# The last batch of an attention loop: values two pairs behind the scores, and its projection split around the last pair

## The chip, the cores and the metric

One core of one Trainium2 chip runs the whole kernel as one program. The metric is device microseconds (us) of one execution. The engines are PE (TensorE matmul; PEld is its weight load), DVE (VectorE), ACT (ScalarE), POOL (GpSimd) and SP (SyncE, which here only issues DMAs). Each works through its own instructions in the order written and waits on semaphores for the others.

## The reference

Two layers over 16 batches of 256 tokens with width 256. The first layer is a conditioned feed-forward block. The second is attention with 16 heads, then a mixture of eight experts. The change is in the attention:

```python
q = _ln(qkv[:, :, 0].transpose(0, 2, 1, 3), qn_g, qn_b)
k = _ln(qkv[:, :, 1].transpose(0, 2, 1, 3), kn_g, kn_b)
v = qkv[:, :, 2].transpose(0, 2, 1, 3)
scores = jnp.einsum('bhnd,bhmd->bhnm', q, k) / jnp.sqrt(jnp.float32(HD))
attn = jax.nn.softmax(scores, axis=-1)
o = jnp.einsum('bhnm,bhmd->bhnd', attn, v)
o = o.transpose(0, 2, 1, 3).reshape(b, n, H * HD)
x = x + o @ Wout.T
tok = x.reshape(-1, d)
gate = jax.nn.softmax(tok @ Wgate.T, axis=-1)
vals, idx = jax.lax.top_k(gate.T, k_cap)
```

The expert choice (`top_k` over all 4096 tokens) needs the gates of every batch, so nothing of the experts can start before the last batch's `x` and its logits are done.

## The kernel before

There are three stages: the first layer (`first_block`), `attention`, and `experts` (which begins with the choice of tokens, called the router here). Each is a block of its own with a barrier between.

`attention` walks over t = -2 to 17. Step t has PAIRS = 8 pair steps s, one for each pair of heads. In pair step s of step t the engines do, for batch t and pair s:

- PE: `scores` (8 matmuls into two score banks, waits for `exped`, the exponentials of the pair before), then `transposes` of the pair before (waits for `shared`), then `values` of that same pair (waits for `pT_act` and `pT_dve`, the two copies of the transposed probabilities).
- DVE: `lowest_of` (the minimum, one per side), `invert` (reciprocal of the sum, one per side), the copy of one transposed bank (`pT_dve`), and `o_l`, the low part of the output.
- ACT: `exps` (four exponentials, each with the read of its accumulator), then the copy of the other transposed bank (`pT_act`), and `o_h`, the high part of the output.
- POOL: `divide` for side 0 and side 1 (`shared`).

Every fp32 product is made of three float32r products of high and low parts (`product`). In earlier steps the holes between these are filled with work of later batches: the products that make q, k and v (`chunk`), and their transposes. For t = 15, the last batch, there is no later batch, so these pair steps hold little else. What one bank `tr` passes through is fixed by a table of slots 0 to 15, two per pair step (`TR_FILLS`, shifted by `TR_LAG`):

```python
TR_FILLS = [("x2", 0, 1), ("gates", 0, 3), ("proj", 0, 4), ("qk", 0, 5), ("qk", 1, 6), ("qk", 2, 7), ("h", 0, 8), ("qk", 3, 9),
            ("proj", 1, 10), ("qk", 4, 11), ("qk", 5, 12), ("qk", 6, 13), ("qk", 7, 14)]
TR_LAG = {"h": 2, "proj": -1, "x2": -2, "gates": -2, "qk": 1}
```

So batch b's output projection (`project`, 24 matmuls for each half n) runs in step b + 1 at s = 2 and s = 5; ACT copies each half to `proj`, POOL adds both halves to the row tile `x2` at s = 6 (`x2_done`), and the transposes of `x2` and the gate products follow in step b + 2. DVE takes the statistics of `x2`, POOL the root, DVE the normalised rows `x2n`, and SP stores them. For batch 15 these are steps 16 and 17, with no scores beside them. Under all of this SP loads 256 KB pieces of expert weights, ACT and DVE split them (`ew_h` at even s, `ew_l` at odd s) and SP stores them again. Batch 15's `x2` tile is first loaded with the rows of the first layer (`x1_again_in`).

Of the kernel before, what the change touches and what calls it, by code (L numbers as in the profile page):

```python
# [23 lines left out]
P = 128  # L24
# [824 lines left out]
def attention(nc, exponent, weights, rows_of, banks, ident, x1_rows, hbias, cols, x2_rows, logit, out, a, halves, sbuf, sems):  # L849
# [4 lines left out]
    with s:  # L854
# [31 lines left out]
        def first(b):  # L886

            return isinstance(b, int) and b == 0

        drained = {"h": out_h, "proj": out_proj, "x2": out_x2, "gates": out_gates, "qk": out_qk}  # L890
# [31 lines left out]
        with nc.Block() as block:  # L922
            @block.sync
            def _(sp):
# [22 lines left out]
                def step(t, odd):  # L947
                    pieces(t, (0,))
                    b = t - 2
                    if live(b):  # L950
                        wait(sp, out_normed, TT, b, TT)
                        sp.dma_start(x2_rows[bass.ds(b * T, T), :].rearrange("(t p) d -> p t d", p=P), x2n[:, :, :]).then_inc(x2n_stored, 16)
                    b = t - 1
                    if live(b):
                        wait(sp, tr_x2, 1, b - 1, 1)
                        wait(sp, x2_stored, 16, b - 1, 16)
                        wait(sp, out_normed, TT, b - 1, TT)
                        sp.dma_start(x2[:, :, :], x1_rows[bass.ds(b * T, T), :].rearrange("(t p) d -> p t d", p=P)).then_inc(x1_again_in, 16)
                    pieces(t, (1,))
                    b = t + 3  # L960
                    if live(b):
                        wait(sp, tr_h, 1, b - 1, 1)
                        sp.dma_start(x1[:, :, :], x1_rows[bass.ds(b * T, T), :].rearrange("(t p) d -> p t d", p=P)).then_inc(x1_in, 16)
                    pieces(t, (2,))
                    b = t - 1
                    if live(b):
                        wait(sp, x2_done, 1, b, 1)
                        sp.dma_start(out[bass.ds(b * T, T), :].rearrange("(t p) d -> p t d", p=P), x2[:, :, :]).then_inc(x2_stored, 16)
                    pieces(t, (3,))
# [6 lines left out]
            def _(pe):  # L976
# [11 lines left out]

                def transposes(b, q):
                    for side in range(2):  # L990
                        wait(pe, shared, H, b, 2 * q + side + 1)
                        for m in range(TT):
                            for n in range(TT):
                                last = nc.tensor.transpose(pT_bank[side][:, m * T + n * P:m * T + (n + 1) * P],  # L994
                                                           prob[q % 2 * 2 + side][:, n, m * P:(m + 1) * P], ident[:, :])
                        last.then_inc(pT_done, 1)

                def values(b, q, its):
                    wait(pe, pT_act, PAIRS, b, q + 1)
                    wait(pe, pT_dve, PAIRS, b, q + 1)  # L1000
                    wait(pe, o_lo, PAIRS, b, q)
                    if q == 0:
                        wait(pe, chunk_out, 12, b, 12)
                    for m in range(TT):
                        for side in range(2):
                            h = 2 * q + side
                            last = nc.tensor.matmul(o_bank[side * HD:(side + 1) * HD, 0:T], v[its][:, m, h * HD:(h + 1) * HD],  # L1007
                                                    pT[q % 2 * 2 + side][:, m, :], start=(m == 0), stop=(m == TT - 1))
# [21 lines left out]
                def fill(t, i):  # L1030
# [7 lines left out]
                    if name == "x2":  # L1038
                        wait(pe, x2_done, 1, b, 1)
                    if name == "gates":  # L1040
# [16 lines left out]
                    if name == "gates":  # L1057
# [4 lines left out]
                        last.then_inc(tr_gates, 1)  # L1062

                def step(t, odd):
                    for s in range(PAIRS):
                        b, q, its = pair_at(t, s, 1, odd)
                        if live(t):
# [8 lines left out]
                        if name == "proj" and live(c):  # L1076
                            project(t, c, n, 1 - odd)
                        if live(b):
                            values(b, q, its)
                        fill(t, 2 * s + 1)  # L1080
# [3 lines left out]
            def _(act):  # L1084
# [10 lines left out]
                def empty(b, name, j, its):  # L1095
# [9 lines left out]
                    if name == "qk":  # L1105
                        wait(act, tr_qk, 8, b, j + 1)
                        if isinstance(b, int) and b == 1:
# [4 lines left out]
                                             bias=cols[:, g + 1:g + 2], scale=cols[:, g:g + 1]).then_inc(out_qk, 1)  # L1112
                    if name == "proj":
                        wait(act, tr_proj, TT, b, j + 1)
# [24 lines left out]
                def step(t, odd):  # L1139
                    for s in range(PAIRS):  # L1140
                        b, q, its = pair_at(t, s, 2, odd)
                        if live(b):
                            wait(act, pv_done, PAIRS, b, q + 1)
                            if q == 0:
                                wait(act, tr_proj, TT, b - 2, TT)
                            nc.scalar.activation(o_h[its][:, q, :], o_bank[:, 0:T], ACT.Copy).then_inc(o_hi, 1)
                        empty(*fill_at(t, 2 * s - 1), 1 - odd)
# [21 lines left out]
            def _(pool):  # L1169
# [18 lines left out]
                def step(t, odd):  # L1188
                    far, new, old = t + 2, t + 1, t - 1
                    for s in range(PAIRS):  # L1190
# [7 lines left out]
                        if live(old) and s == X2_PAIR:  # L1198
                            wait(pool, out_proj, TT, old, TT)
# [14 lines left out]
            def _(dve):  # L1214
# [35 lines left out]
                def out_norm(t, s, part):  # L1250


                    if s == OUT_STATS_PAIR and live(t - 1):
                        if part < TT:
                            wait(dve, x2_done, 1, t - 1, 1)
                            link.note(nc.vector.bn_stats(out_stats[:, part, :], x2[:, part, :]))
# [8 lines left out]
                    if s == OUT_APPLY_PAIR and live(t - 2) and part < TT:  # L1265
                        wait(dve, out_root, 1, t - 2, 1)
# [20 lines left out]
                def step(t, odd):  # L1287
                    far = t + 2
                    for s in range(PAIRS):
                        i = 2 * s  # L1290
                        before = chunks_at(t, s - 1)
                        if live(t):
                            lowest_of(t, s, 0)
                            lowest_of(t, s, 1)
                        b, q, its = pair_at(t, s, 2, odd)
                        if live(b):
                            wait(dve, o_hi, PAIRS, b, q + 1)
                            nc.vector.tensor_tensor(o_l[its][:, q, :], o_bank[:, 0:T], o_h[its][:, q, :].bitcast(F32), ALU.subtract).then_inc(o_lo, 1)
                        if live(t):
# [516 lines left out]
```

## Time and profile before

| | us |
|---|---|
| median of 3 runs | 1573.68 (1571.06 to 1573.81) |
| the profiled execution's own time | 1573.23 |
| span of its trace | 1571.3 |
| scores of batch 15, pair 1, begin | 1217.82 |
| `x2` of batch 15 complete (DVE's statistics begin) | 1279.44 |
| first router instruction on DVE | 1284.89 |

The span is what the trace covers. The execution's own time is 1.93 us longer. Times of an instruction are from the span's start. The page gives the granted TensorE clock as a share of full speed: 1.00 is 2.4 GHz, 0.50 is 1.2 GHz.

### The profile page before, as it was taken

The page shows a single profiled execution, that of the slowest core. Times are in us where ns is not written, and L with a number is a line of the kernel's source. Part 1 is how long each engine was busy: PE and PEld are TensorE (multiplying, and loading weights), DVE is VectorE, ACT ScalarE, POOL GpSimd, SP SyncE. Part 2 cuts the span into 40 slices and gives each one's busy share as a digit, 9 for nine tenths or more (in the row PEclk, how much of TensorE's full clock was granted, in tenths as well). Part 3 has the DMA queues.
Part 4 walks back from the last instruction along what each step waited for, and adds up shares of the span by engine and source line. Part 5 has one row for each costly group of instructions (what it writes and reads, how often), then busy time and mean ns, then how long its engine had stood idle before and what let it go on. Part 6 is the DMA issues. An engine that isn't in the chain of part 4 may idle for free. (4 is left out here: it accounts for less than half of the span.)

```text
span 1571.3 us, 31208 instructions
## 1 busy us (share of the span) xinstructions
PE 1390.1 (88%) x9672; PEld 1138.5 (72%) x9672; DVE 1019.1 (65%) x2493; ACT 960.7 (61%) x2537; POOL 783.9 (50%) x737
## 2 busy tenths in 40 slices
PE   1599999997899999999999999999998752599996
PEld 1589999995567777777777777777776542498996
DVE  2686667644677776777777677767766446565642
ACT  2266655564777777777877877787776510335452
POOL 1376666653345545654564565556545310255633
PEclk9799999998999999999999999999999875699999
DMA  7122222210122222222221222222222234067652
GB/s 233 41 65 67 63 71 61 54 42 27 41 67 80 83 63 76 87 81 75 80 82 60 74 87 81 81 74 88 75 68 81 81 126 165 27 201 226 207 170 27
DMA packets 92408, 138.90 MB, mean 88 GB/s; under 512 B 8656, under 2 KB 61824, under 8 KB 92160
## 3 DMA queue, kind: packets, MB, share of 16 engines
q1 hardware_dynamic: 83600, 126.02, 24.2%
q0 software_dynamic: 6144, 8.39, 2.9%
q10 hardware_dynamic: 2544, 3.16, 0.6%
q8 instruction: 42, 0.69, 0.2%
q14 instruction: 78, 0.64, 0.1%
HBM read 87.20 MB, written 50.35 MB: 88 GB/s over the span
## 5 line engine op out<-in xcount | busy, mean ns | idle before, releaser
L1182 POOL TENSOR_TENSOR prob<-prob,share_p 128x512 f32<-128x512 f32 x256 | 268.0, 1053 | 342.0 <-DVE share_p L1285 342.0
L1091 ACT ACTIVATE prob<-bank,shift 128x256 f32<-128x256 f32 x512 | 236.0, 474 | 115.4 <-DVE shift L1279 115.2
L1279 DVE TENSOR_REDUCE shift<-bank 128x2 f32<-128x512 f32 x256 | 164.7, 685 | 207.4 <-PE bank L984 202.2
L1177 POOL TENSOR_TENSOR raw_qk<-raw_qk,rq 128x512 f32<-128x512 f32 x128 | 145.5, 1149 | 65.3 <-DVE rq L100 65.3
L1007 PE MATMUL bank<-pT,v 128*64 128x256 f32 x1024 | 141.1, 397 | 36.0 <-ACT pT L1154 35.1
L147 PE MATMUL bank<-wqkv_h,rowsT_h 128*128 128x512 f32 x384 | 161.1, 420 | 4.3 <-PEq L392 3.5
L147 PE MATMUL bank<-wqkv_h,rowsT_l 128*128 128x512 f32 x384 | 152.2, 396 | 0.0
L147 PE MATMUL bank<-wqkv_l,rowsT_h 128*128 128x512 f32 x384 | 151.9, 396 | 0.0
L984 PE MATMUL bank<-landing 64*128 64x256 f32 x1024 | 149.2, 411 | 0.4 <-ACT prob L1091 0.4
L994 PEld LDWEIGHTS bank<-ident,prob 128*128 128x128 f32 x1024 | 111.1, 142 | 44.5 <-issue 42.8
L994 PE MATMUL bank<-ident,prob 128*128 128x128 f32 x1024 | 142.2, 282 | 0.4 <-POOL prob L1182 0.4
L1007 PEld LDWEIGHTS bank<-pT,v 128*64 128x64 f32 x1024 | 62.8, 137 | 93.5 <-ACT pT L1154 42.1
L984 PEld LDWEIGHTS bank<-landing 64*128 64x128 f32 x1024 | 90.4, 191 | 32.5 <-issue 24.6
L1110 ACT ACTIVATE landing<-bank,cols 128x512 f32<-128x512 f32 x128 | 102.3, 799 | 11.0 <-PE bank L1050 11.0
L1091 ACT ACTIVATION_READ_ACCUMULATOR prob<-bank,shift 128x1 f32 x512 | 104.2, 204 | 0.0
L630 POOL TENSOR_TENSOR hid_l<-hid,hid_h 128x512 fp32r<-128x512 f32 x64 | 86.0, 1353 | 32.4 <-ACT hid_h L547 31.7
L1132 ACT ACTIVATE raw_sq<-bank 128x512 f32<-128x512 f32 x128 | 79.4, 620 | 30.0 <-DVE ssq L1275 30.0
L543 ACT ACTIVATE hid<-bank,cols 128x256 f32<-128x256 f32 x128 | 53.4, 471 | 68.9 <-PE bank L147 68.9
L1275 DVE TENSOR_REDUCE ssq<-raw_sq 128x8 f32<-128x512 f32 x128 | 86.1, 675 | 6.2 <-ACT raw_sq L1132 4.6
L1305 DVE COPY pT<-bank 128x512 f32<-128x512 f32 x128 | 88.0, 688 | 0.4 <-issue 0.3
L1050 PE MATMUL bank<-ident,raw_qk 128*128 128x128 f32 x512 | 81.8, 283 | 5.8 <-ACT landing L1110 4.4
L147 PEld LDWEIGHTS bank<-wqkv_h,rowsT_h 128*128 128x128 f32 x384 | 73.4, 191 | 18.1 <-issue 4.0
(279 smaller groups left out, 4052.7 us busy)
## 6 DMA issues: line engine op xcount, KB each, us to landing
ew_raw<-in_fc1s SPq DMA_DIRECT2D x32, 256.0 KB, 3.3
split_w1h<-ew_h SPq DMA_DIRECT2D x32, 256.0 KB, 2.0
split_w1l<-ew_l SPq DMA_DIRECT2D x32, 256.0 KB, 2.5
ew_raw<-in_fc2s SPq DMA_DIRECT2D x32, 256.0 KB, 2.9
split_w2h<-ew_h SPq DMA_DIRECT2D x32, 256.0 KB, 2.1
split_w2l<-ew_l SPq DMA_DIRECT2D x32, 256.0 KB, 2.6
ew_h<-split_w1h SPq DMA_DIRECT2D x8, 1024.0 KB
ew_l<-split_w1l SPq DMA_DIRECT2D x8, 1024.0 KB
```

Source lines behind the costliest of these rows:

```text
L147: last = nc.tensor.matmul(out, a, b, start=(n == 0), stop=(n == 3 * len(ks) - 1))
L630: nc.gpsimd.tensor_tensor(hid_l[:, 2 * g:2 * g + 2, :], hid[:, 2 * g:2 * g + 2, :], hid_h[:, 2 * g:2 * g + 2, :].bitcast(F32), ALU.subtrac ...
L984: mm = nc.tensor.matmul(score_bank[side][:, n * T:(n + 1) * T], qT[odd][r, s, n * P:(n + 1) * P], kT[odd][r, s, :], start=True, stop=True)
L994: last = nc.tensor.transpose(pT_bank[side][:, m * T + n * P:m * T + (n + 1) * P], prob[q % 2 * 2 + side][:, n, m * P:(m + 1) * P], ident[: ...
L1007: last = nc.tensor.matmul(o_bank[side * HD:(side + 1) * HD, 0:T], v[its][:, m, h * HD:(h + 1) * HD], pT[q % 2 * 2 + side][:, m, :], start= ...
L1091: last = nc.scalar.activation(prob[at][:, n, :], score_bank[side][:, n * T:(n + 1) * T], ACT.Exp, bias=shift[:, at, n:n + 1], scale=-1.0, ...
L1110: nc.scalar.activation(dst[its][:, j % 2 * 4:j % 2 * 4 + 4, j // 4 * P:(j // 4 + 1) * P], tr[:, :].rearrange("p (m n) -> p m n", m=4), ACT ...
L1177: nc.gpsimd.tensor_tensor(part, part, rq[:, n, c * 8:(c + 1) * 8].unsqueeze(2).to_broadcast([P, 8, HD]), ALU.mult).then_inc(normed, 1)
L1182: nc.gpsimd.tensor_tensor(prob[at][:, :, :], prob[at][:, :, :], share[:, at, :].unsqueeze(2).to_broadcast([P, TT, T]), ALU.mult).then_inc( ...
L1275: nc.vector.tensor_reduce(ssq[:, n, c * 8:(c + 1) * 8], raw_sq[c % 2][:, :].rearrange("p (h d) -> p h d", h=8), AX, ALU.add).then_inc(summ ...
L1279: nc.vector.tensor_reduce(shift[:, s % 2 * 2 + side, :], score_bank[side][:, :].rearrange("p (n m) -> p n m", n=TT), AX, ALU.min).then_inc ...
L1305: nc.vector.tensor_copy(pT[q % 2 * 2 + 1][:, :, :].rearrange("p m n -> p (m n)"), pT_bank[1][:, :]).then_inc(pT_dve, 1)
```

## The change

Only batch 15 (`closing`) and the steps 16 and 17 behind it change.

1. `values` of batch 15 run two pair steps behind the scores, not one. Odd pairs write to `chunk_bank[1]`, even ones to `o_bank`; a bank's next write waits for `o_l` of two pairs before. `transposes` gets an explicit wait for both copies of the pair before, which `values` used to imply. `o_h` and `o_l` follow one pair step later (`taken_at`).
2. Step 16 on PE is written out (`finish`). The projection of batch 15 goes to two banks of its own (`last_proj`), both halves n, for pairs 0 to 5 before the values of pair 7, then pair 6, then pair 7.
3. DVE adds each half straight from PSUM to `x2`; the two copies on ACT and the add on POOL are gone for batch 15. The normalised rows of batch 14 move ahead from s = 2 to s = 1 of step 16.

```diff
+def values_at(t, s, odd):
+    if isinstance(t, int) and t == NB - 1:
+        return [(t - 1, PAIRS - 1, 1 - odd)] if s == 0 else [(t, s - 2, odd)] if s > 1 else []
+    return [pair_at(t, s, 1, odd)]
+
+def taken_at(t, s, odd):
+    if isinstance(t, int) and t == NB - 1:
+        return [pair_at(t, s, 2, odd)] if s < 2 else [(t, s - 3, odd)] if s > 2 else []
+    if isinstance(t, int) and t == NB:
+        return [(t - 1, q, 1 - odd) for q in {0: (PAIRS - 3, PAIRS - 2), 2: (PAIRS - 1,)}.get(s, ())]
+    return [pair_at(t, s, 2, odd)]
...
+        last_proj = chunk_bank[0], score_bank[0]
+        def values_bank(b, q):
+            return chunk_bank[1] if closing(b) and q % 2 else o_bank
...
                 def transposes(b, q):
+                    if isinstance(b, int) and b == NB - 1:
+                        wait(pe, pT_act, PAIRS, b, q)
+                        wait(pe, pT_dve, PAIRS, b, q)
...
                 def values(b, q, its):
-                    wait(pe, o_lo, PAIRS, b, q)
+                    wait(pe, o_lo, PAIRS, b, max(q - 1, 0) if closing(b) else q)
...
+                def project_last(ks, its):
+                    for n in range(TT):
+                        for k in ks:
+                            if n == 0:
+                                wait(pe, o_lo, PAIRS, NB - 1, k + 1)
+                            oh, ol = (o[its][:, k, n * P:(n + 1) * P] for o in (o_h, o_l))
+                            for i, (l, r) in enumerate(((oh, wo_h), (oh, wo_l), (ol, wo_h))):
+                                last = nc.tensor.matmul(last_proj[n][:, 0:D], l, r[:, k, :], start=(k == 0 and i == 0),
+                                                        stop=(k == PAIRS - 1 and i == 2))
+                        if k == PAIRS - 1:
+                            last.then_inc(tr_proj, 1)
...
+                def finish(t, its):
+                    fill(t, 1)
+                    values(t - 1, PAIRS - 2, its)
+                    transposes(t - 1, PAIRS - 1)
+                    wait(pe, exped, H, t - 1, H)
+                    project_last(range(PAIRS - 2), its)
+                    fill(t, 3)
+                    values(t - 1, PAIRS - 1, its)
+                    project_last((PAIRS - 2,), its)
+                    project_last((PAIRS - 1,), its)
...
+                        if closing(t - 1) and s == 3:
+                            wait(dve, x1_again_in, 16, t - 1, 16)
+                            for n in range(TT):
+                                wait(dve, tr_proj, TT, t - 1, n + 1)
+                                nc.vector.tensor_tensor(x2[:, n, :], last_proj[n][:, 0:D], x2[:, n, :], ALU.add).then_inc(out_proj, 1)
```

**PE, pair step s = 1 of step 15.** The transposes of pair 0 (`bank<-ident,prob`), then before the change its values (`bank<-pT,v`), the gate products of batch 13 and the scores of pair 2:

```order
L994 MATMUL bank<-ident,prob 128x128 [waits shared]
L994 MATMUL bank<-ident,prob 128x128 x3
L994 MATMUL bank<-ident,prob 128x128 [waits shared]
L994 MATMUL bank<-ident,prob 128x128 x3
L1007 MATMUL bank<-pT,v 64x256 [waits o_lo,chunk_out,pT_dve,pT_act]
L1007 MATMUL bank<-pT,v 64x256 x3
L1060 MATMUL bank<-wgate,proj 128x8 [waits out_x2]
L1060 MATMUL bank<-wgate,proj 128x8 x3
L984 MATMUL bank<-landing 128x256 [waits exped]
L984 MATMUL bank<-landing 128x256 x3
```

The same place after the change:

```order
L1032 MATMUL bank<-ident,prob 128x128 [waits shared,pT_dve,pT_act]
L1032 MATMUL bank<-ident,prob 128x128 x3
L1032 MATMUL bank<-ident,prob 128x128 [waits shared]
L1032 MATMUL bank<-ident,prob 128x128 x3
L1112 MATMUL bank<-wgate,proj 128x8 [waits out_x2]
L1112 MATMUL bank<-wgate,proj 128x8 x3
L1019 MATMUL bank<-landing 128x256 [waits exped]
L1019 MATMUL bank<-landing 128x256 x3
```

The values are gone from between the transposes and the next scores. They stand one pair step later, behind the next transposes, and the transposes name two more semaphores.

**PE, the end of step 15 and the start of step 16.** Before, the values of pair 6, the transposes and values of pair 7, then the transposes of batch 14's `x2` and its gates:

```order
L1007 MATMUL bank<-pT,v 64x256 [waits o_lo,pT_dve,pT_act]
L1007 MATMUL bank<-pT,v 64x256 x3
L994 MATMUL bank<-ident,prob 128x128 [waits shared]
L994 MATMUL bank<-ident,prob 128x128 x3
L994 MATMUL bank<-ident,prob 128x128 [waits shared]
L994 MATMUL bank<-ident,prob 128x128 x3
L1007 MATMUL bank<-pT,v 64x256 [waits o_lo,pT_dve,pT_act]
L1007 MATMUL bank<-pT,v 64x256 x3
L1055 MATMUL bank<-ident,x 128x128 [waits out_proj,x2_done]
L1055 MATMUL bank<-ident,x 128x128 x3
L1060 MATMUL bank<-wgate,proj 128x8 [waits out_x2]
L1060 MATMUL bank<-wgate,proj 128x8 x3
```

After, the values of pair 5, the transposes of `x2`, the values of pair 6 and the transposes of pair 7, up to the first projection matmuls of batch 15 (`bank<-wout_h,o_h`):

```order
L1045 MATMUL bank<-pT,v 64x256 [waits o_lo,pT_dve,pT_act]
L1045 MATMUL bank<-pT,v 64x256 x3
L1107 MATMUL bank<-ident,x 128x128 [waits out_proj,x2_done]
L1107 MATMUL bank<-ident,x 128x128 x3
L1045 MATMUL bank<-pT,v 64x256 [waits o_lo,pT_dve,pT_act]
L1045 MATMUL bank<-pT,v 64x256 x3
L1032 MATMUL bank<-ident,prob 128x128 [waits shared,pT_dve,pT_act]
L1032 MATMUL bank<-ident,prob 128x128 x3
L1032 MATMUL bank<-ident,prob 128x128 [waits shared]
L1032 MATMUL bank<-ident,prob 128x128 x3
L1064 MATMUL bank<-wout_h,o_h 128x256 [waits o_lo,exped]
L1064 MATMUL bank<-wout_l,o_h 128x256
```

Values come a pair later: those of pair 6 stand behind batch 14's `x2` transposes. 36 projection matmuls follow the transposes of pair 7 instead of its values.

**DVE, step 16.** Before, up to the statistics of batch 15's rows, which wait for POOL's add (`x2_done`):

```order
L1298 TENSOR_TENSOR o_l<-bank,o_h 128x256 [waits o_hi]
L1305 COPY pT<-bank 128x512 [waits pv_done,pT_done]
L1298 TENSOR_TENSOR o_l<-bank,o_h 128x256 [waits o_hi]
L1268 TENSOR_SCALAR x2n<-x,out_moment,out_rstd 128x256 [waits x2n_stored,out_root] x2
L1256 BN_STATS out_stats<-x 128x6 [waits x2_done] x2
L1261 BN_AGGR out_moment<-out_stats 128x2 [waits att_links]
L1261 BN_AGGR out_moment<-out_stats 128x2
```

After, with the two adds from PSUM (`x<-bank,x`) on DVE itself:

```order
L1365 TENSOR_TENSOR o_l<-bank,o_h 128x256 [waits o_hi] x2
L1377 COPY pT<-bank 128x512 [waits pv_done,pT_done]
L1335 TENSOR_SCALAR x2n<-x,out_moment,out_rstd 128x256 [waits x2n_stored,out_root] x2
L1365 TENSOR_TENSOR o_l<-bank,o_h 128x256 [waits o_hi]
L1370 TENSOR_TENSOR x<-bank,x 128x256 [waits tr_proj,x1_again_in]
L1370 TENSOR_TENSOR x<-bank,x 128x256 [waits tr_proj]
L1323 BN_STATS out_stats<-x 128x6 [waits out_proj] x2
L1328 BN_AGGR out_moment<-out_stats 128x2 [waits att_links]
L1328 BN_AGGR out_moment<-out_stats 128x2
```

The statistics now wait for DVE's own adds (`out_proj`), each of which waits for its half of the projection (`tr_proj`).

## Rows read from the trace of the kernel before

**Rows 1.** Page: span and PE; chain that ended last, first piece (start us, us).

```profile
span 1571.3 us, 31208 instructions
PE 1390.1 (88%) x9672; PEld 1138.5 (72%) x9672; DVE 1019.1 (65%) x2493; ACT 960.7 (61%) x2537; POOL 783.9 (50%) x737
...
1349.22 0.30 issue
```

**Rows 2.** Windows of PE, one pair step each: length, busy, clock, DMA share, GB/s.

```profile
1217.82:1225.57 7.75, 5.54 (x33) 0.80 0.28 88
1225.57:1233.32 7.75, 7.75 (x49) 0.75 0.18 56
1233.32:1238.70 5.38, 3.17 (x27) 1.00 0.12 42
...
1257.27:1279.44 22.17, 15.97 (x102) 0.86 0.14 48
sum 61.62, PE 46.59; mean PE 6.66
```

**Rows 3.** Timeline of PE, pair steps 1 and 3: start us, us, instruction, [idle before].

```profile
1217.82 1.14 PE L984 MATMUL bank<-landing 64*128 64x256 f32 x8
...
1233.32 1.13 PE L984 MATMUL bank<-landing 64*128 64x256 f32 x8
1234.38 1.09 PE L994 MATMUL bank<-ident,prob 128*128 128x128 f32 x8
1237.68 1.08 PE L1007 MATMUL bank<-pT,v 128*64 128x256 f32 x8 [2.21 <-ACT pT L1154]
```

**Rows 4.** Timelines of DVE, ACT and POOL, pair steps 3, 4 and 7.

```profile
1234.48 1.29 DVE L1279 TENSOR_REDUCE shift<-bank 128x2 f32<-128x512 f32 x2 [3.19 <-PE bank L984]
...
1261.84 0.74 DVE L1256 BATCH_NORM_STATS2 out_stats<-x 128x6 f32<-128x256 f32 x2
...
1235.21 0.47 ACT L1091 ACTIVATE prob<-bank,shift 128x256 f32<-128x256 f32 x1 [1.39 <-DVE shift L1279]
...
1236.93 0.21 ACT L1091 ACTIVATION_READ_ACCUMULATOR prob<-bank,shift 128x1 f32 x1
1237.02 0.61 ACT L1154 ACTIVATE pT<-bank 128x512 f32<-128x512 f32 x1
...
1236.51 2.49 POOL L1182 TENSOR_TENSOR prob<-prob,share_p 128x512 f32<-128x512 f32 x2 [4.09 <-DVE share_p L1285]
1241.89 2.04 POOL L1182 TENSOR_TENSOR prob<-prob,share_p 128x512 f32<-128x512 f32 x2 [2.89 <-DVE share_p L1285]
```

**Rows 5.** Timeline of PE, pair steps 4 and 5, at half clock.

```profile
1243.06 1.98 PE L1007 MATMUL bank<-pT,v 128*64 128x256 f32 x8 [2.21 <-ACT pT L1154]
1244.97 1.84 PE L984 MATMUL bank<-landing 64*128 64x256 f32 x8
```

**Rows 6.** Timeline of PE, pair step 5: first of 24 projection matmuls, then the values.

```profile
1247.59 0.37 PE L147 MATMUL bank<-wout_h,o_h 128*128 128x256 f32 x1
...
1250.61 1.08 PE L1007 MATMUL bank<-pT,v 128*64 128x256 f32 x8
```

**Rows 7.** Timelines of PE, DVE and POOL behind pair 7's scores.

```profile
1265.56 1.08 PE L1007 MATMUL bank<-pT,v 128*64 128x256 f32 x8 [0.88 <-DVE pT L1305]
...
1268.01 1.03 PE L1060 MATMUL bank<-wgate,proj 128*128 128x8 f32 x8 [0.78 <-ACT proj L1119]
...
1267.09 0.42 DVE L1298 TENSOR_TENSOR o_l<-bank,o_h 128x256 fp32r<-128x256 f32 x1 [1.64 <-ACT o_h L1146]
...
1279.44 0.75 DVE L1256 BATCH_NORM_STATS2 out_stats<-x 128x6 f32<-128x256 f32 x2 [11.28 <-POOL x L1201]
...
1278.15 1.26 POOL L1201 TENSOR_TENSOR x<-proj,x 128x512 f32<-128x512 f32 x1 [13.06 <-ACT proj L1116]
```

**Rows 8.** Timelines of SP and DVE: rows loaded for batch 15, the router's start.

```profile
1268.68 0.41 SPq L958 DMA_DIRECT2D x<-x_rows  x1
...
1284.89 0.42 DVE L1445 TENSOR_REDUCE peak<-logit 128x32 f32<-128x256 f32 x1 [2.65 <-PEq L922]
```

More of the change, by code:

```diff
@@ L888, in first, with closing, wait_x2 @@
             return isinstance(b, int) and b == 0
+        last_proj = chunk_bank[0], score_bank[0]
+        def closing(b):
+            return isinstance(b, int) and b == NB - 1
+        def values_bank(b, q):
+            return chunk_bank[1] if closing(b) and q % 2 else o_bank
+        def wait_x2(eng, b):
+            if closing(b):
+                wait(eng, out_proj, TT, b, TT)
+            else:
+                wait(eng, x2_done, 1, b, 1)
         drained = {"h": out_h, "proj": out_proj, "x2": out_x2, "gates": out_gates, "qk": out_qk}
@@ L1006, in values @@
                             h = 2 * q + side
-                            last = nc.tensor.matmul(o_bank[side * HD:(side + 1) * HD, 0:T], v[its][:, m, h * HD:(h + 1) * HD],
+                            last = nc.tensor.matmul(values_bank(b, q)[side * HD:(side + 1) * HD, 0:T], v[its][:, m, h * HD:(h + 1) * HD],
                                                     pT[q % 2 * 2 + side][:, m, :], start=(m == 0), stop=(m == TT - 1))
@@ L1038, in fill @@
                     if name == "x2":
-                        wait(pe, x2_done, 1, b, 1)
+                        wait_x2(pe, b)
+                        if closing(b):
+                            wait(pe, out_gates, 1, b - 1, 1)
                     if name == "gates":
@@ L1062, in fill @@
                         last.then_inc(tr_gates, 1)
+                def finish(t, its):
[8 more added lines that the diff above has]
+                    project_last((PAIRS - 1,), its)
                 def step(t, odd):
+                    if isinstance(t, int) and t == NB:
+                        finish(t, 1 - odd)
+                        return
                     for s in range(PAIRS):
-                        b, q, its = pair_at(t, s, 1, odd)
+                        b, q, _ = pair_at(t, s, 1, odd)
                         if live(t):
@@ L1077, in step @@
                             project(t, c, n, 1 - odd)
-                        if live(b):
-                            values(b, q, its)
+                        for b, q, its in values_at(t, s, odd):
+                            if live(b):
+                                values(b, q, its)
                         fill(t, 2 * s + 1)
@@ L1112, in empty @@
                                              bias=cols[:, g + 1:g + 2], scale=cols[:, g:g + 1]).then_inc(out_qk, 1)
-                    if name == "proj":
+                    if name == "proj" and not closing(b):
                         wait(act, tr_proj, TT, b, j + 1)
@@ L1140, in step @@
                     for s in range(PAIRS):
[L1141 to L1146, printed above, removed]
+                        for b, q, its in taken_at(t, s, odd):
+                            if live(b):
+                                wait(act, pv_done, PAIRS, b, q + 1)
+                                if q == 0:
+                                    wait(act, tr_proj, TT, b - 2, TT)
+                                nc.scalar.activation(o_h[its][:, q, :], values_bank(b, q)[:, 0:T], ACT.Copy).then_inc(o_hi, 1)
                         empty(*fill_at(t, 2 * s - 1), 1 - odd)
@@ L1197, in step @@
                             nc.gpsimd.tensor_tensor(rstd[:, :], var_eps[:, :], exponent[:, :].to_broadcast([P, TT]), ALU.pow).then_inc(spread_out, 1)
-                        if live(old) and s == X2_PAIR:
+                        if live(old) and not closing(old) and s == X2_PAIR:
                             wait(pool, out_proj, TT, old, TT)
@@ L1254, in out_norm @@
                         if part < TT:
[L1255 removed]
+                            wait_x2(dve, t - 1)
                             link.note(nc.vector.bn_stats(out_stats[:, part, :], x2[:, part, :]))
@@ L1264, in out_norm @@
                             nc.vector.tensor_scalar(out_var[:, :], out_moment[:, :, 1], LN_EPS, None, ALU.add).then_inc(out_spread, 1)
-                    if s == OUT_APPLY_PAIR and live(t - 2) and part < TT:
+                    if s == (1 if closing(t - 1) else OUT_APPLY_PAIR) and live(t - 2) and part < TT:
                         wait(dve, out_root, 1, t - 2, 1)
@@ L1294, in step @@
                             lowest_of(t, s, 1)
[L1295 to L1298, printed above, removed]
+                        for b, q, its in taken_at(t, s, odd):
+                            if live(b):
+                                wait(dve, o_hi, PAIRS, b, q + 1)
+                                nc.vector.tensor_tensor(o_l[its][:, q, :], values_bank(b, q)[:, 0:T], o_h[its][:, q, :].bitcast(F32), ALU.subtract).then_inc(o_lo, 1)
+                        if closing(t - 1) and s == 3:
[3 more added lines that the diff above has]
+                                nc.vector.tensor_tensor(x2[:, n, :], last_proj[n][:, 0:D], x2[:, n, :], ALU.add).then_inc(out_proj, 1)
                         if live(t):
```

2 lines of the change are left out of this document (1 added, 1 removed).

## The prediction

> **What bounds the kernel now.** The page comes first: PE is busy 88% of 1571.3 us, more than any other engine, but the chain that ended last reaches back only to 1349.22 [rows 1]. It says nothing of the attention, so the stretch that is changed has to be read by itself. The front gives the fixed points. From the router's first DVE instruction at 1284.89 [rows 8] to the end of the span are 286.41 us that the change leaves alone. The router needs the last logits and the last stored rows, so whatever batch 15 gains in front of it moves the end by as much.
>
> The windows of PE give batch 15. From the scores of pair 1 at 1217.82 to the complete `x2` at 1279.44 are 61.62 us, in which PE is busy 46.59 [rows 2]. The reader is to see three things. Pair step 3, which holds nothing extra and runs at full clock, takes 5.38 us with PE busy for 3.17. The steps with gates or a projection take 7.75. The tail from pair 7's scores on takes 22.17.
>
> Why 5.38? The timelines of one pair step show it. Scores start at 1233.32 [rows 3], the minimum at 1234.48, the exponentials at 1235.21, and the last accumulator read ends at 1236.93 + 0.21 = 1237.14, which is 3.82 after the scores began. Only then does ACT copy the transposed bank, ending at 1237.02 + 0.61 = 1237.63 [rows 4], and 0.05 later the values start, after PE waited 2.21 [rows 3]. The next scores stand behind the values in PE's order. So the loop is scores, minimum, exponentials, copy, values. PE isn't short of time. Its order makes the scores wait for a copy that they don't need.
>
> **The change part by part.** I follow PE in absolute time S, the start of each pair's scores, first at full clock.
>
> *Ordinary pair steps.* With the values of the pair before last, whose copies are long done, the next scores wait only for the exponentials: 3.82 + 0.05 (the semaphore's delay seen above) = 3.87 in place of 5.38. PE must fit into it. Scores take 1.06 (1233.32 to 1234.38 [rows 3]). In the new order pair 4's scores would have begun at 1237.14 + 0.05 = 1237.19. Side 1 of pair 3's transposes needs the second divide, which ends at 1236.51 + 2.49 = 1239.00 [rows 4], 1.81 later. Half the transposes is 0.55, and values are 1.02 (5.38 less 4.36, the values' start). That is 1.81 + 0.55 + 1.02 = 3.38, so 0.49 is spare. Where no weight split runs beside POOL, two divides take 2.04 and more is spare. The added wait for copies costs nothing: they end 0.49 after the exponentials, while scores take 1.06. Queued behind that wait are the values, which have the same slack. The gates of step 1 (1.03 [rows 7]) fill a hole that was a wait.
>
> *Steps with half of batch 14's projection.* Here PE's own work is longer than the loop. 24 matmuls take 1250.61 - 1247.59 = 3.02 [rows 6]. Pair step 2: 1.81 + 0.55 + 3.02 + 1.02 = 6.40. Pair step 5 has the shorter divides before it. They end at 1241.89 + 2.04 = 1243.93 [rows 4], 1.41 after their exponentials (1238.70 + 3.82 = 1242.52), so side 1 goes right behind side 0: 1.06 + 1.09 + 3.02 + 1.02 = 6.19.
>
> *Sum to pair 7.* From S1 = 1217.82: +3.87 (S2), +6.40 (S3), +3.87, +3.87 (S5), +6.19 (S6), +3.87 gives S7 = 1245.89.
>
> *The tail.* Values of pair 6 start at S7 + 4.36, when their copies are done. They take 1.02 and transposes of pair 7 1.09, which makes 6.47. The two statistics of batch 14 (0.74) delay pair 7's second divide to about S7 + 5.97 (1243.93 - 1238.70 = 5.23, and 0.74 [rows 4]), when side 0 of the transposes is just done: nothing. Then 36 matmuls at 3.02/24 = 4.53, at S7 + 11.00. Gates of batch 14: 1.03. Values of pair 7, then `o_h` on ACT and `o_l` on DVE: 1265.56 to 1267.51, 1.95 [rows 7], with pair 6's six matmuls hidden under the two. With 0.05 for the semaphore, S7 + 14.03. Pair 7's six matmuls: 0.13 apart and 0.28 for the last give 0.91. Each add on DVE from PSUM is new; the nearest row is `o_l`, of the same shape and also from PSUM, 0.42. The first hides under the second half's matmuls. So `x2` is complete at S7 + 14.03 + 0.91 + 0.05 + 0.42 + 0.05 = S7 + 15.46 = 1261.35. The old hand-over, a copy on ACT and POOL's 1.26 [rows 7], is gone. Bounds of an add: it can't be below nothing, nor above POOL's 1.26 for both halves, so -0.4 to +0.8.
>
> *Moved work.* The normalised rows of batch 14 go ahead on DVE, and behind them SP loads batch 15's rows (issued at 1268.68 before [rows 8]). In the new order DVE reaches them behind pair 7's copy, about S7 + 8, and the load is issued 0.5 later. The adds want it near S7 + 14, so nothing; if this cover were gone, each microsecond late would cost one. The pieces of expert weights keep their places in the pair steps. ACT's `ew_h` may wait for its piece in the shorter steps. Behind it stand only `o_h` and the next exponentials, which have over 1 us, and the steps concerned (5 and 7) are bound by PE or by the tail. I take nothing, bound 1. Instructions on PE are the same in number.
>
> *Clock.* 1279.44 - 1261.35 = 18.09 at full clock. Before, the granted clock was 0.75 to 0.86 of full in the windows with gates or the tail and 1.00 in pair step 3 [rows 2], so some falls to 1.2 GHz lie in the old 61.62. At half clock, after a wait of 2.21, values took 1.98 and scores 1.84 where they take 1.08 and 1.13 at full [rows 5, 3]: one such fall costs 1.66. The new order has no such waits inside the pair steps, but it has the gates in steps 1 and 2, the small waits of the tail, and the projection in step 2 right behind. I take one fall left on PE's chain: 18.09 - 1.66 = 16.4. Bounds: none, and three (5.0).
>
> The Trainium skill, page "TensorE: Matmul & The Clock Gate", section on HAM oscillation, says that idle gaps between bursts throttle the clock, and that closing them keeps it full. By that rule alone no fall would be left and the sum would be 18.1; this is a rival below. The trace agrees that falls follow waits, but also shows 0.75 in the window in which PE is never idle [rows 2], so the row leaves one.
>
> The skill's page "SBUF — State Buffer", section "SBUF: two separate sides", says a DVE instruction with two SBUF inputs and a GpSimd one exclude each other for the whole instruction. By that the split on DVE could hold a divide back by more than the 0.45 in the rows (2.49 against 2.04), and PE's 0.49 spare could run out. The sum goes by the row.
>
> **Sum.** 1573.23 (the profile's own time, 0.03% below the median of 1573.68) less 16.4 gives 1556.8.
>
> **The rivals.**
>
> - *As worked out*, one or two falls of the clock: 1555 to 1559. Chance 0.50.
> - *Clock full throughout*: 1573.23 - 18.1 = 1555.1, or a little less where the tail's last gates gain too. For it: the waits of 2.21 are gone. Against it: pair step 2. Chance 0.20.
> - *Clock falls three times*: 1573.23 - 18.1 + 5.0 = 1560.1. For it: gates leave PE at half clock in the old steps 1 and 2. Chance 0.13.
> - *The pair step doesn't shorten* since another wait takes the place of the copy: the second divide, or ACT behind a late weight piece. Then four steps stay 1.51 longer each, and the gain is 18.1 - 1.7 - 6.0 = 10.4: 1562.8. Against it: 0.49 and more are spare. Chance 0.10.
> - *It doesn't do what it says*, no change: something else than `x2` holds the router back, such as the stores of expert weights. Against it: DVE's statistics waited 11.28 for `x2` [rows 7] with DVE and ACT nearly idle. Chance 0.04.
> - *Slower*: PE stays at 1.2 GHz from pair 1 to `x2`. Then PE's own work counts. Rows 5 against rows 3 give 1.84/1.13 and 1.98/1.08, about 1.75 times as long. Six steps of 3.17 become 33.3, the two halves of the projection 10.6, and the tail 15.46 + 0.75 x 10.6 (what of it is PE's) = 23.4: 67.3 for 61.62, so 1578.9. Half clock costs about 0.5 us for each microsecond of it on PE's chain, so it decides from some 36 of the 43.5 new ones. Against it: PE ran at full clock through pair step 3, with a wait in it. Chance 0.03.
>
> **How the numbers follow.** Predicted is the likeliest, 1556.8. The first three hold 0.83 between 1554 and 1561; with the bounds on the adds, on `ew_h` and on unseen semaphore delays the range is 1554.0 to 1561.5. About 0.2%, 3 us, is what a measurement of this kernel tells from no change. Faster by more: all but the last two cases, 0.93; within: 0.04; slower: 0.03.
>
> **What would show it.** In the trace after: scores of pairs 3 and 4 3.9 apart, with no PE wait for the ACT copy in between; scores of pair 3 about 6.4 behind those of pair 2; pair 7's scores near 1246 to 1248; 36 projection matmuls in one run at 0.13 each; DVE's adds near 0.42; statistics of batch 15 near 1261 to 1263; the router's start 5.45 behind them as now. The prediction is wrong if PE waits for the second divide, if the granted clock stays at 0.5 for long, if the adds wait for the load of rows, or if router and experts take other than 286.4.

## The result

| | us |
|---|---|
| before, median of 4 runs | 1572.37 (1570.52 to 1573.81) |
| after, median of 4 runs | 1554.24 (1553.39 to 1556.56) |
| ratio after / before | 0.9875 (95% interval 0.9852 to 0.9898) |
| span of the profiled execution, before / after | 1571.3 / 1551.9 |

The change made the kernel faster by 18 us, clearly more than a measurement can miss. The ratio is not the quotient of the two medians, which is 0.9885 and lies inside the interval. The forecast was 1556.8, in a range from 1554.0 to 1561.5. The median lies 0.2 us above the range's lower bound; 0.9875 of the 1572.37 would be 1552.7, below it. So the direction and the wait that was named hold, and the gain was forecast too small: 16.4 us, where the two profiled executions differ by 1573.23 - 1554.05 = 19.2.

The page of the changed kernel answers to [rows 1]:

```profile
span 1551.9 us, 31212 instructions
PE 1380.8 (89%) x9672; PEld 1132.0 (73%) x9672; DVE 1019.5 (66%) x2495; ACT 959.8 (62%) x2535; POOL 783.3 (50%) x736
```

The windows of PE, one for each pair step, then the tail, the end of the stage, and router with experts, answer to [rows 2]. Columns: from:to, length, busy, granted clock, DMA share, GB/s:

```profile
1217.17:1221.05 3.88, 2.95 (x26) 1.00 0.00 0
1221.05:1227.34 6.29, 6.16 (x48) 1.00 0.48 161
1227.34:1231.22 3.88, 3.17 (x26) 1.00 0.25 83
1231.22:1235.10 3.88, 3.39 (x25) 1.00 0.51 173
1235.10:1241.08 5.98, 5.98 (x49) 1.00 0.11 42
1241.08:1244.95 3.87, 3.17 (x26) 1.00 0.75 236
1244.95:1259.97 15.02, 13.82 (x108) 1.00 0.20 71
1259.97:1265.41 5.44, 1.72 (x12) 0.71 0.27 96
1265.41:1551.90 286.49, 217.03 (x1528) 0.85 0.49 152
```

From pair 1's scores to the statistics of batch 15 (called the stretch from here on) are 1259.97 - 1217.17 = 42.80 us, where they were 61.62: 18.82 less. The pair step that took 5.38 takes 3.88. The rest of the 19.4 between the two spans is 0.65 in front of the stretch (1217.82 to 1217.17). What lies behind it is as long as before, 5.44 + 286.49 against 5.45 + 286.41. And the clock reads 1.00 in all seven windows of the stretch in this trace.

PE's timeline of one pair step shows what bounds it now:

```profile
1231.22 1.13 PE L1019 MATMUL bank<-landing 64*128 64x256 f32 x8 [0.71 <-ACT prob L1158]
1232.29 1.45 PE L1032 MATMUL bank<-ident,prob 128*128 128x128 f32 x8
1233.66 1.08 PE L1045 MATMUL bank<-pT,v 128*64 128x256 f32 x8
1235.10 1.13 PE L1019 MATMUL bank<-landing 64*128 64x256 f32 x8 [0.35 <-ACT prob L1158]
```

The wait of 2.21 for ACT's copy [rows 3] is gone. What is left is a wait for the exponentials (`prob`) in front of the scores, 0.35 to 0.93, four times in the stretch. The transposes at 1232.29 take 1.45 for 1.09: their second side waits inside the group for POOL's second divide, which ends at 1233.02, and the later wait is shorter by as much (0.35 for 0.71). PE's spare time beside a weight split is this 0.35, where the prediction had 0.49.

The tail, on PE and DVE, answers to [rows 7]:

```profile
1249.32 1.08 PE L1045 MATMUL bank<-pT,v 128*64 128x256 f32 x8 [0.61 <-ACT pT L1221]
1250.33 1.09 PE L1032 MATMUL bank<-ident,prob 128*128 128x128 f32 x8
1251.18 0.37 PE L1064 MATMUL bank<-wout_h,o_h 128*128 128x256 f32 x1
...
1255.54 0.95 PE L1112 MATMUL bank<-wgate,proj 128*128 128x8 f32 x8
1256.42 1.08 PE L1045 MATMUL bank<-pT,v 128*64 128x256 f32 x8
...
1258.45 0.39 PE L1064 MATMUL bank<-wout_h,o_h 128*128 128x256 f32 x1
...
1257.97 0.42 DVE L1365 TENSOR_TENSOR o_l<-bank,o_h 128x256 fp32r<-128x256 f32 x1 [4.79 <-ACT o_h L1213]
1259.18 0.76 DVE L1370 TENSOR_TENSOR x<-bank,x 128x256 f32<-128x256 f32 x2 [0.78 <-PE bank L1064]
1259.97 0.75 DVE L1323 BATCH_NORM_STATS2 out_stats<-x 128x6 f32<-128x256 f32 x2
```

The 36 projection matmuls run from 1251.18 to 1255.54 without a hole. Pair 7's six begin at 1258.45, as soon as DVE's low part is there. Two adds from PSUM take 0.76, the first beside the second half's matmuls.

### The profile page after: what moved, and what is told of

Read it like the earlier page. It is cut to its first block and busy times, and to the rows that moved or that the text cites. A ratio compares the mean times of both kernels' runs of the same rounds, so it can differ in the third digit from the quotient of the medians.

```text
span 1551.9 us, 31212 instructions
## 1 busy us (share of the span) xinstructions
PE 1380.8 (89%) x9672; PEld 1132.0 (73%) x9672; DVE 1019.5 (66%) x2495; ACT 959.8 (62%) x2535; POOL 783.3 (50%) x736
```

## The experiments

The first theory was that two things had been mixed in one number: PE's order (the copy in front of the scores), and a clock that falls because of the waits this order makes. The rival was that falls (of the granted clock from 1.00 to 0.50) come by chance whatever the order, and that the full clock after the change was luck. A second rival was that the split projection, not the lag of the values, gave most of the gain. All stretches below are from one profiled execution of each kernel; times are medians, ratios are against runs of the kernel before on the same chip. The experiments ran on two chips (`proj_warm` and `both` on the second), beside 11, 10 and 9 runs of before with medians of 1573.59, 1575.85 and 1574.61.

| kernel | pair 1 to 7 | tail | stretch | median us | ratio (95%) |
|---|---|---|---|---|---|
| before | 39.45 | 22.17 | 61.62 | 1572.37 | |
| after | 27.78 | 15.02 | 42.80 | 1554.24 | 0.9875 (0.9852 to 0.9898) |
| after_again | 27.75 | 15.01 | 42.76 | 1554.07 | 0.9873 (0.9836 to 0.9909) |
| lag_only | 28.68 | 20.38 | 49.06 | 1559.39 | 0.9909 (0.9890 to 0.9928) |
| proj_only | 43.21 | 18.04 | 61.25 | 1565.58 | 0.9964 (0.9943 to 0.9986) |
| before_warm | 34.38 | 19.71 | 54.09 | 1566.93 | 0.9948 (0.9926 to 0.9970) |
| proj_warm | 34.46 | 15.46 | 49.92 | 1561.66 | 0.9920 (0.9890 to 0.9949) |
| copy_add | 27.74 | 16.25 | 43.99 | 1555.09 | 0.9881 (0.9861 to 0.9900) |
| one_bank | 27.95 | 19.04 | 46.99 | 1557.44 | 0.9891 (0.9855 to 0.9926) |
| split_scores | 26.64 | 15.14 | 41.78 | 1553.63 | 0.9866 (0.9839 to 0.9893) |
| early_proj | 28.82 | 13.73 | 42.55 | 1554.08 | 0.9868 (0.9840 to 0.9896) |
| both | 27.76 | 13.88 | 41.64 | 1554.95 | 0.9874 (0.9849 to 0.9899) |

**Each part alone.** `lag_only` keeps the first edit and takes back the split and the adds:

```diff
-                    wait(pe, exped, H, t - 1, H)
-                    project_last(range(PAIRS - 2), its)
                     fill(t, 3)
                     values(t - 1, PAIRS - 1, its)
-                    project_last((PAIRS - 2,), its)
-                    project_last((PAIRS - 1,), its)
+                    project(t, t - 1, 0, its)
+                    project(t, t - 1, 1, its)
...
```

> Only the values two pairs behind the scores, with the two banks in turn. The projection of batch 15 stays whole behind pair 7's values, copied by ACT and added by POOL. If PE's order made the scores wait for the copy, pair steps 3 and 4 are 3.88 us as after the change, pair 1's scores to pair 7's scores take 27.8 (39.45 before), and the stretch from pair 1's scores to the statistics of batch 15 takes about 46 (61.62 before, 42.80 after), so about 1557 us. If most of the gain came from the projection's split instead, pair steps stay near 5.4 and the stretch is near 56.

The time is 14.2 us below the 1573.59 of before beside it. The pair steps behind the first are those of after. The stretch, expected at about 46, is 3 us longer: the clock was down twice, at pair 1's scores (window 1217.92 to 1222.70, clock 0.81, 4.78 us for 3.88) and in the tail with the projection (0.92), and the gates waited 0.83 for ACT.

`proj_only` keeps the split and the adds, and puts the values back to one pair behind:

```diff
 def values_at(t, s, odd):
     if isinstance(t, int) and t == NB - 1:
-        return [(t - 1, PAIRS - 1, 1 - odd)] if s == 0 else [(t, s - 2, odd)] if s > 1 else []
+        pass
     return [pair_at(t, s, 1, odd)]
...
```

`taken_at` goes back as well, and all values write to `o_bank` again.

> Only the projection of batch 15 in two banks with six parts ahead of the last values, and the adds on DVE; values stay one pair behind. Pair steps stay 5.38 or more; behind pair 7's scores the tail is near 15.8 us in place of 22.2, the stretch about 55, and the time about 1566 us. If the split's six parts only move work that was not on the path, the tail stays above 20.

The median is as expected. The stretch was not: 61.25 for 55. The profiled execution was the second longest of its seven (1573.44, where they range from 1564.32 to 1574.25), and its windows say why. First two pair steps:

```profile
1217.82:1226.62 8.80, 6.59 (x33) 0.69 0.26 80
1226.62:1235.51 8.89, 8.89 (x50) 0.64 0.23 69
```

The order in these pair steps is that of before, where they took 7.75 each, yet they are 1.1 us longer, and the clock is 0.11 lower. This is the first row that shows the clock as a thing that varies from run to run while the waits are there. The tail is 4.1 shorter than before, 18.04 for the expected 15.8, at a clock of 0.83.

**The clock by itself.** `before_warm` is the kernel before with work for PE in its waits, and nothing else. In an ordinary pair step 0.77 of the 2.21 is left idle (5.37 long, 4.60 busy):

```diff
                 def values(b, q, its):
+                    if isinstance(b, int) and b == NB - 1 and q not in (1, 4):
+                        if q == 0:
+                            wait(pe, chunk_out, 12, b, 12)
+                        for i in range(12 if q < PAIRS - 1 else 4):
+                            nc.tensor.matmul(chunk_bank[1][:, 0:D], wo_h[:, i % 8, 0:P], wo_h[:, i % 8, :], start=True, stop=True)
```

> The kernel before, with 12 extra matmuls (256 columns, into a bank nobody reads) on PE in each wait for the copy in batch 15, four in the last, none where a projection stands there. They fit into the wait of 2.21 us (12 x 0.13 = 1.5), so the order of the work is that of before and only PE's idleness is gone. If the falls of the clock came from those waits, the granted clock stays near 1.00, ordinary pair steps are all 5.4, and the stretch is 55 to 57 us for 61.62: 5 to 6 us faster. If the falls have nothing to do with the waits, the stretch stays 60 to 63 and the time is that of before.

64 matmuls were added and the kernel became faster by 0.5%; the stretch gained 7.5 us where 5 to 6 were expected. Its windows:

```profile
1219.04:1225.40 6.36, 5.59 (x45) 1.00 0.12 44
1225.40:1231.35 5.95, 5.95 (x49) 1.00 0.35 105
1231.35:1236.73 5.38, 4.60 (x39) 1.00 0.28 79
1236.73:1242.10 5.37, 4.60 (x38) 1.00 0.44 146
1242.10:1248.05 5.95, 5.95 (x50) 1.00 0.06 22
1248.05:1253.42 5.37, 4.60 (x38) 1.00 0.56 174
1253.42:1273.13 19.71, 15.04 (x118) 1.00 0.16 54
```

Pair steps are 5.37 and 5.38, the length of the old order, all at full clock. So the order costs 5.38, and the falls had cost 61.62 - 54.09 = 7.5 us of the old stretch in the traced execution. From pair 2's scores to pair 7's scores the rival of chance falls is out: all eight traces of the new order read 1.00 there.

Chance is left at pair 1's scores, which still have the wait of 2.21 in pair step 0 in front of them. Five of the eight traces of the new order read 1.00 in that window, two met half clock (0.81 in `lag_only`, 0.79 in `early_proj`) and one in part (`both`, 0.96). Up to that window `early_proj` has the same order on PE as after, and this is its row:

```profile
1216.89:1221.71 4.82, 3.90 (x25) 0.79 0.00 0
```

So the same wait was followed by a fall in one execution and by none in another, and such a fall cost 0.9 us (4.82 and 4.78 for 3.88).

`proj_warm` adds the same matmuls to `proj_only` (to pairs 0, 2, 3, 5 and 6):

```diff
...
+                    if isinstance(b, int) and b == NB - 1 and q not in (1, 4, PAIRS - 1):
...
+                        for i in range(12):
...
```

> The split projection and DVE's adds alone, values one pair behind, with 12 extra matmuls in each wait for the copy where no projection stands. If proj_only lost its gain only to falls of the clock, all windows up to pair 7's scores read 1.00, those pair steps together take 34.4 us as in before_warm (43.2 in proj_only's trace), the tail is 15 to 16, and the stretch about 50: 4 us less than before_warm's 54.1, at about 1563. If splitting itself makes pair steps longer, they stay above 36 with a full clock.

As expected: 34.46 and 15.46 at clock 1.00. Now the 18.82 us can be laid out in a row, each term the difference of two traces. The falls cost 7.5 (before to `before_warm`), the split with the adds gives 54.09 - 49.92 = 4.2, and the values' lag gives 49.92 - 42.80 = 7.1.

**The adds.** `copy_add` is the changed kernel with ACT's copies and POOL's add:

```diff
-                    if name == "proj" and not closing(b):
+                    if name == "proj":
...
-                        nc.scalar.activation(proj[:, j, :], tr[:, 0:D], ACT.Copy).then_inc(out_proj, 1)
+                        nc.scalar.activation(proj[:, j, :], (last_proj[j] if closing(b) else tr)[:, 0:D], ACT.Copy).then_inc(out_proj, 1)
...
```

> The changed kernel, but with the halves of batch 15's projection copied by ACT and added by POOL as before. By the rows the hand-over then takes 0.05 + 0.39 + 0.1 + 1.26 + 0.03 = 1.8 us for 0.55: the stretch is 1.3 us longer than after, 44.1, all behind the last projection matmul. If POOL's add was hidden, nothing changes.

The stretch is 1.19 longer than after, for 1.3 expected. POOL and DVE at its end:

```profile
1261.23 1.26 POOL L1265 TENSOR_TENSOR x<-proj,x 128x512 f32<-128x512 f32 x1 [8.09 <-ACT proj L1180]
...
1262.52 0.75 DVE L1320 BATCH_NORM_STATS2 out_stats<-x 128x6 f32<-128x256 f32 x2 [2.81 <-POOL x L1265]
```

So 1.2 of the 4.2 are the adds, and 3.0 is left for the six parts ahead. The medians (1555.09 and 1554.24) can't tell this 1.2 from nothing.

**The second bank.** `one_bank` lets every pair's values use `o_bank`:

```diff
-            return chunk_bank[1] if closing(b) and q % 2 else o_bank
+            return o_bank
...
-                    wait(pe, o_lo, PAIRS, b, max(q - 1, 0) if closing(b) else q)
+                    wait(pe, o_lo, PAIRS, b, q)
```

> The changed kernel with one bank for the values of batch 15: each waits for the low part of the pair before. DVE has that part about 2.9 us behind the scores' start in the trace of after (1.29 for the minimum and 0.42 for the low part behind 1.16), values start about 2.2 to 2.4 behind it, so they wait some 0.5 us, ending near 3.9, just what the pair step has. I expect pair steps 3.9 to 4.0 in place of 3.88, steps with a projection unchanged, and the stretch 0 to 0.5 us longer. If the second bank matters, pair steps go to 4.3 or more and the time by 2 us.

Right for the pair steps, wrong for the stretch, which is 4.2 us longer for 0 to 0.5 expected. In the pair steps the values wait 0.78 for DVE's low part, which moves the next scores by only 0.06. But the values of pair 6 wait 2.18:

```profile
1230.98 1.08 PE L1045 MATMUL bank<-pT,v 128*64 128x256 f32 x8 [0.78 <-DVE o_l L1365]
...
1252.62 0.70 PE L1045 MATMUL bank<-pT,v 128*64 128x256 f32 x2 [2.18 <-DVE o_l L1365]
...
1250.58 0.96 DVE L1331 TENSOR_SCALAR out_var<-out_moment 128x2 f32<-128x2 f32 x1
1251.46 0.68 DVE L1406 TENSOR_TENSOR ew_l<-ew_raw,ew_h 128x512 fp32r<-128x512 f32 x1
1252.06 0.41 DVE L1365 TENSOR_TENSOR o_l<-bank,o_h 128x256 fp32r<-128x256 f32 x1
```

The view ends inside the group at 1252.62, so its row counts two of eight matmuls. DVE does batch 14's statistics and a weight split before pair 5's low part. Without the second bank PE waits for all of it, and the clock falls behind the wait (0.91 in that tail). I had looked only at the ordinary pair step.

**What bounds now, and can it be moved?** `split_scores` issues the scores by side, each behind its own exponentials:

```diff
+                        for side in range(2):
+                            wait(pe, exped, H, t, 2 * s - 1 + side)
+                            r = slice(side * HD, (side + 1) * HD)
+                            for n in range(TT):
...
```

> The changed kernel, but the scores of batch 15 go side by side: side 0 waits for side 0's exponentials alone, side 1 for side 1's. If a pair step is now bound by the loop scores, minimum, exponentials, side 0's scores begin about 0.9 us earlier, and a step falls from 3.88 to PE's and POOL's bound of 3.2 to 3.5: 2 to 3 us over the steps 2, 4, 5 and 7 and the tail. If the order n before side let the two row halves of PE overlap, the scores take up to twice 1.06 and it is slower by 1 us for each step.

The steps behind pairs 1, 3 and 6 fall to about 3.1 (pair 1's scores at 1219.45, pair 2's at 1222.41), but those behind them give most back (7.21 for 6.29, 4.21 for 3.88). The stretch is 1.0 shorter, for 2 to 3 expected. Where nothing waits inside them, eight scores take 1.14 in this order and 1.13 in the other, so the rival of an overlap that is lost is out. PE is now busy 30.90 of the last 31.61 us, in part waiting inside groups.

`early_proj` moves twelve projection matmuls of the first half into PE's idle time:

```diff
+                        if closing(t) and s in (4, 6, 7):
+                            project_last(({4: 0, 6: 1, 7: 2}[s],), odd, (0,))
...
                     fill(t, 1)
+                    project_last((3,), its, (0,))
                     values(t - 1, PAIRS - 2, its)
...
```

> The changed kernel, with three projection matmuls of the first half each moved into PE's idle time of pair steps 4, 6 and 7 (0.35 to 0.71 us in the trace of after) and three more before pair 6's values (idle 0.61). Twelve matmuls leave the tail: 12 x 0.12 = 1.4 us less, stretch 41.4, if they fit into the idle time. If they push the scores behind them, part of it comes back, at most 0.1 per step.

The tail is 1.29 shorter (13.73). The stretch is 42.55 for 41.4 expected, since pair 1's scores met half clock in this trace (the row above), which gave 0.94 back. From pair 2 on the stretch is 37.73 where after has 38.92.

`both` has the two edits in one kernel:

> The changed kernel with both: scores side by side and twelve projection matmuls moved ahead. Alone they took 1.0 and 1.2 us off the stretch. Both want PE's idle time: split scores leave PE 30.9 busy of the last 31.6 us, so the twelve matmuls find almost none, and the two don't add: stretch 41.3 to 41.8. If they add, it is 40.6. Either is below what the medians can tell (some 1 us).

As expected the two don't add: 41.64. All three medians (1553.63, 1554.08, 1554.95) lie within 1 us of the changed kernel's 1554.24 and 1554.07. None is a version that can be called faster.

`after_again` is the changed kernel, profiled a second time:

> The changed kernel once more, for its clock. If the waits of 2.21 us were what let the clock fall, the windows from pair 1's scores to the statistics of batch 15 show 1.00 again and the stretch is 42.8 us within 0.3. If the full clock of the first trace was luck and one fall is usual, this trace has one, and the stretch is near 44.5.

42.76, clock 1.00 in all seven windows of the stretch. So the first trace was no single stroke of luck; at pair 1's scores full clock is what most traces have, not all.

## Where the prediction held, and the step that failed

**What bounded it** held. `before_warm` shows the old order at 5.37 and 5.38 with a clock that never falls, and the changed kernel has 3.87 and 3.88 against 3.87 in the sum.

**Ordinary pair steps, gates, copies' wait, weight pieces.** All as said: the added wait for copies is nowhere in the waits, and the gates fit into the hole of step 1. ACT's `ew_h` of pair step 4 did wait for its load, 0.51, inside the bound of 1 and hidden: the exponentials behind it began at 1236.99, 0.73 behind the minimum's start at 1236.26, as elsewhere.

```profile
1236.04 0.63 ACT L1232 ACTIVATE ew_h<-ew_raw 128x512 fp32r<-128x512 f32 x1 [0.51 <-DMA ew_raw<-in_fc2s]
1236.58 0.37 ACT L1213 ACTIVATE o_h<-bank 128x256 fp32r<-128x256 f32 x1
1236.99 0.47 ACT L1158 ACTIVATE prob<-bank,shift 128x256 f32<-128x256 f32 x1
```

**Steps with a projection** were 6.29 and 5.98 for 6.40 and 6.19. **The tail** was 15.02 for 15.46, since the 36 matmuls began 6.23 behind pair 7's scores for 6.47 and took 4.36 for 4.53, and the gates 0.88 for 1.03; the end from pair 7's first matmul was longer, 1.52 for 1.43. The sum's 43.53 for the stretch at full clock was thus 0.73 us above the measured 42.80.

**The clock is the term that was mis-sized.** The step that failed read "I take one fall left on PE's chain: 18.09 - 1.66 = 16.4". None was left in the stretch, in this trace and in `after_again`. With 0 in its place the sum gives 1573.23 - 18.1 = 1555.1, and the profiled execution took 1554.05. Of the 2.8 us between the forecast gain of 16.4 and the 19.2 of the profiled executions, 1.7 are this term, 0.7 are the shorter stretch and 0.65 lie in front of it; 0.3 behind it goes the other way, nearly all of it outside the traced span.

The price of a fall was off too. By its own rows it is (1.98 - 1.08) + (1.84 - 1.13) = 1.61, not 1.66. The old stretch held four falls (from 1222, 1243, 1256 and 1270 on), which by `before_warm` cost 7.5 together, 1.9 each, and a fall left at pair 1's scores costs 0.9. That place is where the forecast fall does come, in three of the eight traces of the new order, and in neither trace of the changed kernel itself. Had it come in the traced execution, it would have been 0.9 of the 1.66.

The reason I gave for the fall was the window in which PE is never idle and the clock reads 0.75 [rows 2]. That row does not show a fall. Finer windows of the kernel before show where the fall begins:

```profile
1221.00:1222.00 1.00, 0.00 (x0) 1.00 0.00 0
1222.00:1223.00 1.00, 0.82 (x6) 0.77 0.00 0
1223.00:1224.00 1.00, 1.00 (x5) 0.50 0.54 211
...
1229.00:1230.00 1.00, 1.00 (x9) 0.81 0.00 0
...
1236.00:1237.00 1.00, 0.00 (x0) 1.00 0.00 0
1237.00:1238.00 1.00, 0.32 (x4) 1.00 0.00 0
...
1242.00:1243.00 1.00, 0.00 (x0) 1.00 0.00 0
1243.00:1244.00 1.00, 0.94 (x6) 0.51 0.00 0
```

PE stands idle from 1221 to 1222, and the clock goes down within the microsecond in which it starts again, the same at 1243. Up to 1229 the clock merely had not come back. But PE's wait in pair step 3 was as long, 2.21, and no fall followed it: the clock reads 1.00 when PE starts again at 1237. The fall from 1270 on begins 0.9 us into the projection, behind shorter waits of 0.78 and 0.36. So the falls of this stretch came with the waits and went with them, but not behind every wait; which waits are followed by one stays open.

The page "TensorE: Matmul & The Clock Gate" of the Trainium skill, section on HAM oscillation, says that idle gaps between bursts throttle the clock; its result was my rival "clock full throughout", with 1555.1. The gaps that it describes are waits for transfers and longer than the 2.21 here. The traces agree with its direction: 1.00 in the seven windows after the waits were removed, and in the seven of `before_warm`, where they were filled. They do not bear out that every gap throttles, as pair step 3 shows. Of the two readings weighed in the prediction, the row was misread, and the page's came nearer.

The other page of the Trainium skill that was weighed, "SBUF — State Buffer", section "SBUF: two separate sides", could have made PE wait for a divide. The two divides beside a weight split took 2.49 as before, and no separate wait of PE for a divide is in the trace. The sum went by this row, so the page's rule was not put to a test of its own.

**The rivals.** No wait took the copy's place (PE did wait for the second divide, inside the transposes, as the sum's 1.81 has it, and this moved no scores), the router started 5.44 behind the statistics as before, and PE did not stay at half clock. What the prediction named as its proof came in for the waits: scores 3.9 apart, adds 0.76 for two, router and experts 286.49. Its times were too late: pair 7's scores began at 1244.95 for 1246 to 1248, and the statistics at 1259.97 for 1261 to 1263.

What also stays open is the 0.65 us in front of the stretch, where both kernels run the same work. The three profiled executions of after, `after_again` and `early_proj`, with the same work up to there, already begin the stretch at 1217.17, 1217.02 and 1216.89, and `copy_add` at 1218.53.

## What to carry to other kernels

If an engine's order puts a consumer that waits in front of a producer that doesn't, move the consumer one round later and give it a second buffer, before looking for a faster instruction. Price the idle time that goes away twice: once as time, once as the clock that PE loses behind it, and get the second price by filling the waits with work that nobody reads. One trace per kernel doesn't settle the clock: here the same wait was followed by a fall in one execution and by none in another. Where a buffer is shared across rounds, check the round with the longest queue on the releasing engine, not the usual one.

## What was not expected of the hardware

64 useless matmuls made the kernel faster: the stretch fell from 61.62 to 54.09 us and the time by 0.5% (ratio 0.9948, 0.9926 to 0.9970). Where the waits stood, the time also varied more. 34 executions of the kernel before lie between 1568.96 and 1580.35, 11.4 us apart; 8 of the changed kernel lie between 1553.28 and 1556.56, 3.3 apart. Filling the waits alone did the same: the 7 executions of `proj_only` are 9.9 apart, the 4 of `proj_warm` 1.4, and the 5 of `before_warm` 2.9. The counts differ and only one execution of each was traced, so that the falls are the cause is likely but not shown.
